# A two-layer transformer kernel: combining the experts and the second attention as one block

## What is computed

```
x = x + layernorm(lightning_attention(layernorm(x)))
x = x + layernorm(moe(layernorm(x)))          # 16 experts, top 2, and a shared swiglu
x = x + layernorm(window_attention(layernorm(x)))
x = x + layernorm(swiglu(layernorm(x)))       # 1024 wide

# moe:    y = sum of two experts' outputs, weighted, + swiglu_shared(x)
# window: windows of 32 tokens, 16 apart; q has 16 heads of 16, k and v 2 groups
scores = q_window @ k_window.T / 4;  o = softmax(scores) @ v_window
out = o (all windows one behind the other, first 1024 rows) @ Wo + bo
```

## Time and profile before

| | us |
|---|---|
| Median of 3 runs | 1273.26 (1271.2 to 1274.28) |
| The profiled execution | 1272.02 |
| its span, first to last instruction | 1270.2 |
| TensorE busy in the span | 1147.1 (90%) |
| VectorE / ACT / POOL busy | 782.7 / 508.9 / 254.5 |
| TensorE's mean granted clock | 0.946 |

### The profile page before, as it was taken

The page is one execution under the profiler, slowest core; times in us unless marked ns, Lnnn a source line. Parts: engine busy times, 40 slices in busy tenths (PEclk is TensorE's granted clock), DMA queues, the critical chain, the costliest instruction groups (busy, mean ns, idle before and its releaser), DMA issues. The chain is left out here.

```text
span 1270.2 us, 19632 instructions
## 1 busy us (share of the span) xinstructions
PE 1147.1 (90%) x6960; PEld 997.0 (78%) x6960; DVE 782.7 (62%) x1631; ACT 508.9 (40%) x941; POOL 254.5 (20%) x264
## 2 busy tenths in 40 slices
PE   5999999999999999999999858599996269889996
PEld 5988888998989898889989746477765267678886
DVE  5756757575665666574756776544437848686644
ACT  5674443344343434433444543122223344363322
POOL 1111101010110101010100100233327524122211
PEclk9999999999999999999999968799998568989999
DMA  4000001000000000010000070333333051100000
GB/s 141 9 1 34 10 1 42 0 33 8 0 33 8 0 33 8 0 41 0 1 1 1 1 263 21 106 111 108 106 101 102 14 160 38 45 1 1 18 17 34
DMA packets 30826, 52.42 MB, mean 41 GB/s; under 512 B 5712, under 2 KB 20016, under 8 KB 29488
## 3 DMA queue, kind: packets, MB, share of 16 engines
q1 hardware_dynamic: 26672, 40.91, 9.8%
q0 software_dynamic: 4096, 10.75, 3.3%
HBM read 36.70 MB, written 10.49 MB: 37 GB/s over the span
## 5 line engine op out<-in xcount | busy, mean ns | idle before, releaser
L619 POOL TENSOR_TENSOR linear_out_squares<-linear_out_squares,lin_sq 128x512 f32<-128x512 f32 x64 | 91.2, 1426 | 599.4 <-ACT lin_sq L520 596.5
L41 PE MATMUL lin_bank<-keep_xT_hi,lin_w_hi 128*128 128x512 f32 x384 | 155.1, 404 | 2.6 <-DVE keep_xT_lo L230 2.6
L575 DVE TENSOR_TENSOR lin_st<-lin_bank,lin_mask 128x512 f32<-128x512 f32 x64 | 44.3, 691 | 175.6 <-PE lin_bank L430 175.6
L42 PE MATMUL lin_bank<-keep_xT_lo,lin_w_hi 128*128 128x512 f32 x384 | 152.2, 396 | 0.0
L43 PE MATMUL lin_bank<-keep_xT_hi,lin_w_lo 128*128 128x512 f32 x384 | 152.0, 396 | 0.0
L516 ACT ACTIVATE lin_o<-lin_bank 128x512 f32<-128x512 f32 x64 | 38.3, 599 | 191.5 <-PE lin_bank L461 191.5
L457 PE MATMUL lin_bank<-lin_st,lin_v 128*128 128x128 f32 x512 | 94.0, 275 | 0.0
L461 PE MATMUL lin_bank<-lin_qd,lin_state 128*128 128x128 f32 x448 | 87.2, 276 | 0.0
L41 PEld LDWEIGHTS lin_bank<-keep_xT_hi,lin_w_hi 128*128 128x128 f32 x384 | 72.7, 189 | 17.9 <-issue 3.0
L43 PEld LDWEIGHTS lin_bank<-keep_xT_hi,lin_w_lo 128*128 128x128 f32 x384 | 72.3, 188 | 17.7
L42 PEld LDWEIGHTS lin_bank<-keep_xT_lo,lin_w_hi 128*128 128x128 f32 x384 | 72.6, 189 | 14.6
(11 more groups left out here) (355 smaller groups left out, 2818.3 us busy)
## 6 DMA issues: line engine op xcount, KB each, us to landing
lin_raw<-in_wp SPq DMA_DIRECT2D x8, 1024.0 KB, 4.8
sorted_y<-linear_out_acc SPq DMA_DIRECT2D x48, 128.0 KB, 2.1
experts_up_expert_up<-in_wgu SPq DMA_DIRECT2D x16, 352.0 KB, 7.5
experts_down<-in_wdn SPq DMA_DIRECT2D x16, 176.0 KB
keep_x<-in_x SPq DMA_DIRECT2D x4, 512.0 KB, 7.5
lin_raw_out<-in_wop SPq DMA_DIRECT2D x8, 256.0 KB, 2.6
tokens_x<-linear_out_acc SPq DMA_DIRECT2D x4, 512.0 KB, 9.3
linear_out_acc<-in_ffn_up SPq DMA_DIRECT2D x2, 1024.0 KB, 7.1
```

What stands on the lines that cost most here:

```text
L41: nc.tensor.matmul(out, lh, rh, start=first, stop=False, skip_group_check=skip)
L42: nc.tensor.matmul(out, lh, rl, start=False, stop=False, skip_group_check=skip)
L619: pool.tensor_tensor(part, part, sq[:, a, :], ALU.add).then_inc(squares_sb, 1)
```

## The change

The blocks "combining" and "window attention" become one, in which each engine's order is written anew.

1. *Order of tiles.* Gathers go through a ring of eight places (the 9th waits for the 1st to be weighed). First the five tiles of each batch that enter q, k and v (`used`), then the other three of each (`rest`), which are not turned and whose x is not normalised here. The five tiles are turned as 512 columns and a tail of 16 (`pe_turn_tail`).
2. *Projections* of batch 0 come before the turning of batch 1, those of batch 1 before the jobs. ACT makes the copies of v that VectorE made.
3. *Jobs.* v gets four columns of ones, so that the product with v, turned round (probabilities stationary, 68 columns moving), also gives the sums. The exponentials are transposed unscaled; VectorE takes the reciprocals of the sums from a copy of o (`raw_o`), POOL scales o (128x256), VectorE turns it in 32x32 blocks (`dve.transpose`), and it is multiplied by Wo six turns behind its job. The transfers of o and the arranging behind them are gone.
4. *Arranging q* goes to POOL for three of four parts (`arrange(pool, ...)`); the low part of the window weights goes from POOL to VectorE.
5. *The norms for the next block* are placed inside the job loop: scales on POOL behind its jobs 11 and 13, ACT's application in its turn 14, VectorE's addition behind the last scores.
6. *Routing.* ACT evicts the turned x and takes the last attention tiles before it splits the shared weights; VectorE makes their low parts later.
7. Load of the feed-forward weights: behind the moves of q. Some semaphores and tiles are shared or placed elsewhere.

```diff
-                for j in range(J):
-                    net.dve_low(dve, j)
                 norms.dve_low(dve, 0)
                 norms.dve_round(dve, chain, L, lambda half: dve.wait_ge(output.y_ready, 2 * L + half + 1), split=False)
                 norms.dve_low(dve, 1)
                 norms.dve_round(dve, chain, L + 1, split=False)
                 norms.dve_low(dve, 2)
                 norms.dve_low(dve, 3)
+                net.dve_low(dve, 0)
+                net.dve_low(dve, 1)
                 router.dve_shift(dve, chain)
+                net.dve_low(dve, 2)
...
                 router.act_gate(act)
+                norms.act_high(act, 0)
+                output.act_take(act, L, bank[0:2])
                 for j in range(J):
                     net.act_high(act, j)
-                norms.act_high(act, 0)
-                output.act_take(act, L, bank[0:2])
...
+                sp.wait_ge(taken, TT)
+                for n in range(BATCH * RR):
...
+                sp.wait_ge(vdup_sb, BATCH)
+                fetched.load(sp, w["ffn_up"], w["ffn_down"])
 
...
+                        pool.wait_ge(taken, n - RING + 1)
+                    for b, slot in enumerate((keep.slot1, keep.slot2)):
+                        pool.indirect_dma_start(out=got[:, b, n % RING, :], out_offset=None, in_=sorted_y,
+                                                in_offset=bass.IndirectOffsetOnAxis(ap=slot[:, t:t + 1], axis=0)).then_inc(arrived[t], DMA)
+
...
+                arrange(pool, 1)
+                pool.wait_ge(q3_sb[1], 1)
+                for n in range(NJ):
+                    pool.wait_ge(raw_o_sb, n + 1)
+                    pool.wait_ge(inv_sb, n + 1)
+                    if n >= 2:
+                        pool.wait_ge(oP_sb, n - 1)
+                    pool.tensor_tensor(o[n % 2].rearrange("p (j i d) -> p j i d", j=4, d=WD), raw_o[n % 2][:, :, 0:2 * GD].rearrange("p j (i d) -> p j i d", d=WD),
+                                       inv[n % 2][:].rearrange("p (j i o) -> p j i o", j=4, o=1).broadcast_to([P, 4, 2 * WG, WD]), ALU.mult).then_inc(o_sb, 1)
+                    if n in (1, 5):
+                        m = 2 if n == 1 else 3
+                        pool.wait_ge(o_sb, n + 1)
+                        arrange(pool, m)
+                        pool.wait_ge(q3_sb[m], 1)
+                    if n == 11:
+                        before.affine.scale_and_shift(pool, chain, 0)
+                    if n == 13:
+                        turn.affine.scale_and_shift(pool, chain, 0)
+
...
+                def weigh(group, *places):
+                    for i in places:
+                        t = group.tiles[i]
+                        n = ORDER.index(t)
+                        if t // TPS >= SHARED_EARLY:
+                            dve.wait_ge(net.y_sb, 2 * (t // TPS - SHARED_EARLY + 1))
+                        dve.wait_ge(arrived[t], 2 * DMA)
+                        chain.link(dve.scalar_tensor_tensor(y[:, t, :], got[:, 0, n % RING, :], keep.weight1[:, t:t + 1], y[:, t, :], ALU.mult, ALU.add))
+                        dve.scalar_tensor_tensor(y[:, t, :], got[:, 1, n % RING, :], keep.weight2[:, t:t + 1], y[:, t, :], ALU.mult, ALU.add).then_inc(taken, 1)
+                        dve.wait_ge(taken, n + 1)
+                        group.dve_stats(dve, chain, "y", i)
+
...
+                (a, b), (c0, c1) = used, rest
+                net.dve_step(dve, chain, *STEPS[0])
+                weights.dve_low(dve)
+                weigh(a, 0)
+                net.dve_step(dve, chain, *STEPS[1])
+                weigh(a, 1, 2)
+                net.dve_step(dve, chain, *STEPS[2])
+                weigh(a, 3)
+                net.dve_step(dve, chain, *STEPS[3])
+                weigh(a, 4)
+                a.dve_spread(dve, chain, "y")
+                net.dve_step(dve, chain, *STEPS[4])
+                a.dve_scale(dve, chain, "y")
+                weigh(b, 0, 1)
+                net.dve_step(dve, chain, *STEPS[5])
+                a.dve_x(dve, chain)
+                weigh(b, 2)
+                a.dve_scale(dve, chain, "x")
+                weigh(b, 3, 4)
+                b.dve_spread(dve, chain, "y")
+                a.dve_low(dve, turned)
+                b.dve_scale(dve, chain, "y")
+                a.dve_low_tail(dve, turned)
+                weigh(c0, 0, 1)
+                b.dve_x(dve, chain)
+                weigh(c0, 2)
+                b.dve_scale(dve, chain, "x")
+                c0.dve_spread(dve, chain, "y")
+                values(0)
+                weigh(c1, 0)
+                b.dve_low(dve, turned)
+                c0.dve_scale(dve, chain, "y")
+                weigh(c1, 1)
+                b.dve_low_tail(dve, turned)
+                weigh(c1, 2)
+                c1.dve_spread(dve, chain, "y")
+                arrange(dve, 0)
+                c1.dve_scale(dve, chain, "y")
...
+                    if 4 <= i < NJ + 4:
+                        n = i - 4
+                        dve.wait_ge(raw_o_sb, n + 1)
+                        if n >= 2:
+                            dve.wait_ge(o_sb, n - 1)
+                        dve.reciprocal(inv[n % 2][:].rearrange("p (j i) -> p j i", j=4), raw_o[n % 2][:, :, 2 * GD:VS]).then_inc(inv_sb, 1)
+                    if 5 <= i < NJ + 5:
+                        n = i - 5
+                        bb, rr, mq = JOBS[n]
+                        dve.wait_ge(o_sb, n + 1)
+                        if bb and mq == 0 and rr == 0:
+                            dve.wait_ge(v_mm, BATCH)
+                        dve.transpose(oP[:, bb, rr, mq * 4 * 2 * WIN:(mq + 1) * 4 * 2 * WIN], o[n % 2]).then_inc(oP_sb, 1)
...
+                    if i == NJ:
+                        before.add(dve, 0)
+                        dve.wait_ge(before.added, 1)
+                        for half in range(2):
+                            turn.statistics(dve, chain, 0, half)
+                for half in range(2):
+                    before.statistics(dve, chain, 1, half)
...
+                net.act_step(act, *STEPS[0])
+                weights.act_high(act)
+                for step in STEPS[1:4]:
+                    net.act_step(act, *step)
+                a.act_root(act, "y")
+                net.act_step(act, *STEPS[4])
+                net.act_output(act, SHARED_EARLY)
+                a.act_apply(act, "y")
+                net.act_step(act, *STEPS[5])
+                net.act_output(act, SEGS - 1)
+                a.act_root(act, "x")
+                a.act_apply(act, "x")
+                b.act_root(act, "y")
+                a.act_high(act, turned)
+                act.wait_ge(a.added, a.adds())
+                b.act_apply(act, "y")
+                a.act_high_tail(act, turned)
+                b.act_root(act, "x")
+                take(0)
+                act.wait_ge(a.turned, KT + 1)
+                b.act_apply(act, "x")
+                c0.act_root(act, "y")
+                b.act_high(act, turned)
+                act.wait_ge(b.added, b.adds())
+                c0.act_apply(act, "y")
+                b.act_high_tail(act, turned)
+                c1.act_root(act, "y")
+                take(1)
+                act.wait_ge(c0.added, c0.adds())
+                c1.act_apply(act, "y")
...
+                    if i == 14:
+                        before.act_apply(act, 0)
                 turn.act_apply(act, 0)
...
+                    if 6 <= i < NJ + 6 and JOBS[i - 6][1] == RR - 1:
+                        n = i - 6
+                        b, t = JOBS[n][0], pair(n)
+                        pe.wait_ge(oP_sb, n + 1)
+                        if t < 2:
+                            pe.wait_ge(v_sb, BATCH)
+                        else:
+                            pe.wait_ge(y_sb, t - 1)
+                        for a in range(2):
+                            tile = JOBS[n][2] * 2 + a
+                            for rr in range(RR):
+                                last = pe.matmul(bank[6 + t % 2][:, a * HID:(a + 1) * HID], oP[:, b, rr, tile * P:(tile + 1) * P], wo[:, rr, :],
+                                                 start=rr == 0, stop=rr == RR - 1)
                         last.then_inc(y_mm, 1)
```

More of the change, by code:

```diff
@@ L951, in pe_up @@
         toks = slice(g * SEG, (g + 1) * SEG)
-        if g == self.start:
+        if g == self.start and not self.split_before:
             pe.wait_ge(self.up_lo, 2 * j + 2)
@@ L1005, in _ @@
                 chain = Chain(pool, pool_own)
-                for norm in (before, turn, after):
-                    pool.memset(norm.affine.power[:], -0.5).then_inc(norm.affine.powered, 1)
+                pool.memset(after.affine.power[:], -0.5).then_inc(after.affine.powered, 1)
                 before.affine.scale_and_shift(pool, chain, 1)
@@ new lines, in _ @@
+                rest[0].add(pool)
+                move_k(1)
+                rest[1].add(pool)
+                pool.wait_ge(rest[1].added, rest[1].adds())
+                arrange(pool, 1)
```

(8 more changed lines are left out.)

518 lines of the change are left out of this document (269 added, 249 removed).

## The result

| | before | after |
|---|---|---|
| Median | 1273.5 us (1270.1 to 1274.28, 6 runs) | 1262.4 us (1259.5 to 1266.3, 6 runs) |
| Ratio, 95% interval | | 0.9917 (0.9895 to 0.9939) |
| Span of the profiled execution | 1270.2 | 1264.6 |
| TensorE busy | 1147.1 | 1161.6 |

What follows compares the result with a forecast made beforehand. Busy time was read by stage, with TensorE pacing the job loop and an engine chain the combining. Gains of 6.1 (routing), 19.5 (front) and 2.8 (loop) made 28.4, less 2.5 for hand-overs: net 26, 1246 us, range 1233 to 1260.

Steps and rivals of the forecast that it cites:

- The low clock: Rival: the job loop runs at clock 0.75, so 53.5 us become 71; 13 us more, 1259 in total; chance 0.17.
- Loop at full clock: First exponential to the feed-forward's first transpose: 67.9 us instead of 70.7, with TensorE at 2.4 us a job.
- 2.9 us of stalls: Job loop: waits for POOL's copies of q, 1.6 us at job 4's scores and 1.3 before job 2's scaling.
- the knot: Job 14: ACT's norm application waits for POOL's scale, exponential 15 comes about 5.3 us after the subtraction, TensorE stands 6.5.
- Product with v: Job loop: the turned product, 68 columns instead of 128, takes 0.7 us instead of 1.02, bounds 0.55 and 1.0.
- POOL's copies: Job loop: each of POOL's three copies of q (64x2048) takes 4.7 us, bounds 1.8 and 7.8.
- Front: From the experts' end to the first exponential: 80.2 us instead of 99.7, a gain of 19.5.
- Routing: Routing block: earlier evictions end the low pass at 742.1 instead of 748.2; gain 6.1 us, bounds 3 and 6.4.
- Hand-overs: Some sixty hand-overs between engines at 0.04 us, 2.5 us taken off the summed gain.
- faster still: Rival: the loop packs better, POOL's copies under 3 us and the job 14 wait overlapped; 1236 us; chance 0.15.
- slow copies: Rival: POOL's copies of q take 7.8 us, stalls 11.7 against 2.9 counted; 1255 us; chance 0.07.
- routing without effect: Rival: the low passes delay the router's shift as much as the evictions gain; 1252 us; chance 0.06.

Runs made afterwards that it cites:

- wide_product: Changed kernel with the product with v moving 128 columns instead of 68; 1257.2 us, 0.971 of the kernel before, on a chip where the changed kernel took 1273.7.
- bridge_gap: Changed kernel plus four unused 128x256 products in each of turns 1, 2 and 3, product with v still 68 columns; 1249.9 us, 0.981 of the kernel before.
- fill_on_dve_2: Changed kernel with the fills of the spread k and v moved from POOL to VectorE; 1262.8 us, 0.990 of the kernel before.
- bridge_fill_scale: Changed kernel plus three unused wide products in turns 1 and 2, next norm's scale behind POOL's job 9, fills on VectorE; 1243.3 us, 0.974 of the kernel before.
- after_again: The changed kernel itself, run again on another chip; 1273.7 us against 1295.0 of the kernel before, 0.983.

## Why the prediction was wrong

- **The low clock was a rival at 0.17, and it is what happened.** The step of the forecast that failed is its term for TensorE in the loop, 2.4 us a job at full clock: the first eight jobs took 4.65. Two steps of the rival's own working failed with it. The argument against it was "at half clock TensorE itself is the pacer", taken from the loop before, which climbed to full clock under the same scores and transposes. That a TensorE without gaps climbs does not hold for these jobs: 98% busy, 38 us, clock 0.50. The change had made the product of v cheaper in the same stroke (68 columns moved), and the sum booked only the saving. `wide_product` shows that with the old number of columns the clock rises 12 us into the loop, as it had in the kernel before 11 us into it (first exponential 1045.13; clock up at 1056). And the rival's price was mis-sized: a mean clock of 0.75 gave 71 us instead of 53.5; eight jobs of 4.65 instead of 2.4 are 18 us more. Why narrow jobs don't raise the clock is not shown, only that they don't.
- **Loop at full clock:** 67.9 forecast, 68.6 measured in `bridge_gap`, with eight of its twelve unused products in it. The terms were near, and part of the agreement is luck: 2.9 us of stalls that don't exist stand against sixteen jobs each 0.1 us longer than forecast. Terms: output product 1.92 (1.94), block transpose 0.42 (0.39), scale and shift 2.2 (2.0), TensorE's stand at the knot 6.5 (5.78), the exponential 5.3 after the subtraction (5.0). The three steps of a job 2.4 (2.42; 2.51 from job to job where no output product stands between).
- **Product with v:** 0.7 was taken between 0.55 and 1.0; it takes 0.84 to 0.93 from start to start. 128 columns cost 0.05 us a job more. The turned product saves 0.1 us a job on TensorE (0.93 against 1.02); its worth is the sum and the orientation of o.
- **POOL's copies:** 4.7 taken between 1.8 and 7.8, measured 1.89, at the lower bound: the price of a fill of as many elements. The 2.9 us of stalls don't exist. The estimate of 3.1 us was made with a figure that the Trainium skill ("GPSIMD Engine Reference", section "3.1 Elementwise — side-by-side cycle accounting") gives for a tight unrolled loop, 1.8 cycles an element; it doesn't say that this is the price of one input. The same section gives 1.03 for the lightest bodies (k ≤ 2), an estimate of 1.8 us here, and with that the trace agrees.
- **Front, 80.2 forecast, 85.7 measured.** The steps came in the forecast order: root, application, turning, projections. The first projections were 5.3 us late (51.5 us after the block starts instead of 46.2), the second set 4.6, the exponential 5.5. 3.7 of it is the cast (4.0 by `fill_on_dve_2`, where it is gone). The forecast moved POOL's fills into the middle of VectorE's queue and named no cost for that, since POOL had room. 1.0 is the first shared step, which TensorE begins at 1.2 GHz (VectorE is through with it 7.4 us after the block starts, not 6.5). In the rest is the weighing of a tile, 1.37 us from start to start (959.06 to 960.43) and not 1.28; the forecast had ten of them in its chain, 0.9 us.
- **Routing, 6.1 earlier:** right at the place that it named: the logits at 742.86 instead of 748.24, 5.8 us earlier when counted from the start of the stage, and TensorE's idle of 6.40 gone. Wrong was "the experts' end is held fixed and the routing gain is subtracted". The first expert tiles wait for their gathers, TensorE idles 8.1 us before them instead of 7.6 and runs them at 1.2 GHz for 8.6 us, until 821.2, where it was 5.6 us before; 4.1 of the 5.5 us arrive at the next block.
- **The low part of the window weights:** VectorE waited 1.5 us for it, 1.6 forecast.
- **Hand-overs:** 2.5 us were added as a lump, from no row. No run shows them apart; a pace read from start to start, as that of the scores, has them in it already.
- **The price of "faster still"** doesn't add up: 1025.6 + 53.5 + 10 is 1089.1, 4.4 us before 1093.5, so 1242 and not 1236. It changes nothing in the outcome.

The rivals "slow copies" (1255) and "routing without effect" (1252) lay near the result and were both wrong in their mechanism: copies are fast, and the routing edit works.

## What to carry to other kernels

Where a stage makes TensorE's products narrower, ask for its clock before booking the saving: look in the trace at what the engine did when the clock last rose, and whether that work is still there. What happens in the last microseconds before a long stretch of small products can cost more than its own length: here the clock fell 1.9 us behind a gap of 0.81 us, and unused wide products in that gap and the next were worth 14 us. They are tested in one run. Whether the filled gap or the wide work does it would take another run, with narrow products in the gaps. And a fill or a copy moved on POOL is not free because POOL is idle: see which VectorE instructions it will lie beside.

## What the runs showed of the hardware

- **A clock that depends on how the stretch began.** The same narrow jobs, TensorE without a gap in both: 0.50 for 38 us in the changed kernel (from 1027.68 to 1065.81), 1.00 for 18.9 us in `bridge_gap` and 20.9 in `bridge_fill_scale`, until output products come among them. Before the first the clock had fallen at 1026.0; before the others it had not.
- **VectorE's cast waits for POOL's fills.** A cast issued beside the two fills ends 0.28 us behind the second one: 971.41 against 971.13 in the changed kernel; in `bridge_gap` it took 3.55 us from 964.85 and ended at 968.40, against 968.12. An addition of two SBUF operands beside POOL's addition (1.81 us from 1014.24) took 1.96 us instead of 0.48. The Trainium skill ("SBUF — State Buffer", section "Who interferes with whom") says that the two engines share a pair of ports, which one instruction holds to its end, that casts can need it, and that two SBUF inputs contend with a POOL instruction that reads; by that rule the traces agree, but for one detail. It gives the pair to whoever issues first, and in the changed kernel the row of the cast begins 0.18 us before that of the first fill (967.27 and 967.45); in `bridge_gap` the fill is first (964.44 and 964.85). That the cast isn't let in between the two fills is what the traces show.
- **Another chip.** The kernel before took 1295 instead of 1274 us there, and in the changed kernels VectorE stood 7 to 15 us between two instructions of one shared step, at the same place of the program, with TensorE idle for most of it (10.4 of the 12 us from 956 to 968 in `after_again`) and no release that the profile traces. The cause was not found.
